# Shared network of a mixture-of-experts layer: the second product in plain fp32 instead of three passes over rounded and small parts

## The reference, cut to what matters

```python
SI = I * 2                     # I = 176
def _swiglu(gu, inter):
    g, u = (gu[..., :inter], gu[..., inter:])
    return jax.nn.silu(g) * u
...
y = jnp.einsum('eti,eih,te->th', h, w_down, combine)      # the experts
gu_s = x @ shared_gate_up                                  # 256 -> 2 * 352
y = y + _swiglu(gu_s, SI) @ shared_down                    # 352 -> 256
```

## Time and profile before

| | |
|---|---|
| time, median of 3 runs | 1204.62 us |
| lowest and highest | 1197.87 and 1205.65 us |
| span of the profiled execution | 1198.6 us |
| mean granted TensorE clock | 0.973 of full speed |
| PE busy | 1134.0 us (95%) |
| weight loads busy | 993.3 us (83%) |
| DVE busy | 756.3 us (63%) |
| ACT busy | 513.5 us (43%) |
| POOL busy | 240.8 us (20%) |

### The profile page before, as it was taken

The page is one execution under the profiler, slowest core; times in us unless marked ns, Lnnn a source line. Parts: engine busy times, 40 slices in busy tenths (PEclk is TensorE's granted clock), DMA queues, the critical chain, the costliest instruction groups (busy, mean ns, idle before and its releaser), DMA issues. The chain is left out here.

```text
span 1198.6 us, 19843 instructions
## 1 busy us (share of the span) xinstructions
PE 1134.0 (95%) x7044; PEld 993.3 (83%) x7044; DVE 756.3 (63%) x1600; ACT 513.5 (43%) x969; POOL 240.8 (20%) x274
## 2 busy tenths in 40 slices
PE   5999999999999999999999996889999779989997
PEld 4988988988989889889898995667776668878897
DVE  4765665666656647657567578754445975786656
ACT  5576344344443443444434555422222356554322
POOL 1012010110100101101001002033332742322211
PEclk9999999999999999999999997899999958999999
DMA  4001001000001001001000003733333324000001
GB/s 149 10 1 36 10 1 36 9 0 35 9 0 40 4 0 44 0 0 44 0 0 1 1 2 120 228 93 106 106 106 91 95 82 146 1 1 1 19 18 36
DMA packets 29212, 50.33 MB, mean 42 GB/s; under 512 B 5122, under 2 KB 19426, under 8 KB 27874
## 3 DMA queue, kind: packets, MB, share of 16 engines
q1 hardware_dynamic: 24978, 38.68, 9.8%
q0 software_dynamic: 3840, 10.49, 3.3%
q10 hardware_dynamic: 336, 0.39, 0.1%
HBM read 36.70 MB, written 10.49 MB: 39 GB/s over the span
## 5 line engine op out<-in xcount | busy, mean ns | idle before, releaser
L635 POOL TENSOR_TENSOR linear_out_row<-linear_out_row,lin_sq 128x512 f32<-128x512 f32 x64 | 91.3, 1426 | 598.7 <-ACT lin_sq L536 595.7
L42 PE MATMUL lin_bank<-keep_xT_hi,lin_w_hi 128*128 128x512 f32 x384 | 155.4, 405 | 2.6 <-DVE keep_xT_lo L244 2.6
L591 DVE TENSOR_TENSOR lin_st<-lin_bank,lin_mask 128x512 f32<-128x512 f32 x64 | 44.3, 692 | 174.9 <-PE lin_bank L446 174.9
L43 PE MATMUL lin_bank<-keep_xT_lo,lin_w_hi 128*128 128x512 f32 x384 | 152.6, 397 | 0.0
L44 PE MATMUL lin_bank<-keep_xT_hi,lin_w_lo 128*128 128x512 f32 x384 | 152.5, 397 | 0.0
L532 ACT ACTIVATE lin_o<-lin_bank 128x512 f32<-128x512 f32 x64 | 38.3, 598 | 189.9 <-PE lin_bank L477 189.9
L473 PE MATMUL lin_bank<-lin_st,lin_v 128*128 128x128 f32 x512 | 94.0, 275 | 0.0
L42 PEld LDWEIGHTS lin_bank<-keep_xT_hi,lin_w_hi 128*128 128x128 f32 x384 | 72.9, 190 | 17.9 <-issue 3.0
L44 PEld LDWEIGHTS lin_bank<-keep_xT_hi,lin_w_lo 128*128 128x128 f32 x384 | 72.5, 189 | 17.8
L477 PE MATMUL lin_bank<-lin_qd,lin_state 128*128 128x128 f32 x448 | 87.2, 276 | 0.0
L43 PEld LDWEIGHTS lin_bank<-keep_xT_lo,lin_w_hi 128*128 128x128 f32 x384 | 72.8, 189 | 14.8
(11 more groups left out here) (395 smaller groups left out, 2775.9 us busy)
## 6 DMA issues: line engine op xcount, KB each, us to landing
lin_raw<-in_wp SPq DMA_DIRECT2D x8, 1024.0 KB, 4.8
sorted_y<-shared_loaded SPq DMA_DIRECT2D x48, 128.0 KB, 2.1
experts_up_expert_up<-in_wgu SPq DMA_DIRECT2D x16, 352.0 KB, 7.2
keep_x<-in_x SPq DMA_DIRECT2D x4, 512.0 KB, 7.3
lin_raw_out<-in_wop SPq DMA_DIRECT2D x8, 256.0 KB, 2.6
tokens_x<-linear_out_row SPq DMA_DIRECT2D x4, 512.0 KB, 10.6
linear_out_row<-in_ffn_up SPq DMA_DIRECT2D x2, 1024.0 KB, 5.9
tail_q<-tail_qT SPq DMA_DIRECT2D x28, 64.0 KB, 2.0
```

The lines of the kernel that those rows point to most:

```text
L42: nc.tensor.matmul(out, lh, rh, start=first, stop=False, skip_group_check=skip)
L43: nc.tensor.matmul(out, lh, rl, start=False, stop=False, skip_group_check=skip)
L591: dve.tensor_tensor(C4(st[:, a, :]), C4(bank[2 + a][:]), mask[:, a:a + 1, :].broadcast_to([P, TPS, P]), ALU.mult).then_inc(st_sb, 1)
L635: pool.tensor_tensor(part, part, sq[:, a, :], ALU.add).then_inc(squares_sb, 1)
```

## The change

For the shared network, h and the down weights are no longer split. `pe_down_whole` multiplies h by the weights in plain fp32, one `matmul` for each tile of tokens where there were three. Gone are the roundings and rests of h (6 on ACT and 6 on DVE in the first place, 6 and 6, all on DVE, in the second), the three splits of down weights on ACT and DVE, and the buffers for them. The down weights get a tensor of their own (`d`), since routing reuses `loaded`. In return `h` has to live until its down product is done: `dve_product` of step n waits for `down_mm` of step n - 2, where it waited for the rest. In `experts` the product of step 5 moves behind `dve_tokens`. Buffers `h_hi` and `h_lo` shared their place in memory with `oP` in the tail; `oP` now has a place of its own. The feed-forward network keeps the three passes.

```diff
@@ SwigluWeights
-        if fetched is None:
+        self.whole_down = fetched is None
+        if self.whole_down:
             self.loaded = c.sb("loaded", [P, n_up + J * HID + LOADED_PAD])
-            fetched = Fetched(c, widths, self.loaded[:, 0:n_up], self.loaded[:, n_up:n_up + J * HID])
+            self.d = c.sb("d", [P, J, HID])
+            fetched = Fetched(c, widths, self.loaded[:, 0:n_up], self.d[:].rearrange("p j f -> p (j f)"))
...
-        self.d_lo, self.d_hi = c.sb("d_lo", [P, J, HID], F32R), c.sb("d_hi", [P, J, HID], F32R)
+        if not self.whole_down:
+            self.d_lo, self.d_hi = c.sb("d_lo", [P, J, HID], F32R), c.sb("d_hi", [P, J, HID], F32R)
@@ dve_product
         if n >= 2:
-            dve.wait_ge(self.h_sb, n - 1)
+            dve.wait_ge(self.down_mm, n - 1)
@@ new
+    def pe_down_whole(self, pe, g, j):
+
+        n, w = (g - self.start) * self.J + j, self.widths[j]
+        first, count = self.parts[g]
+        if n == 0 and not self.split_before:
+            pe.wait_ge(self.down_in, self.J * DMA)
+        pe.wait_ge(self.product_sb, n + 1)
+        for t in range(count):
+            to = self.bank[4 + (first + t) % TPS // 2][:, t % 2 * HID:(t % 2 + 1) * HID]
+            last = pe.matmul(to, self.h[0:w, n % 2, t * P:(t + 1) * P], self.raw_d[0:w, j, :],
+                             start=j == 0 and t % 2 == 0, stop=j == self.J - 1, skip_group_check=True)
         last.then_inc(self.down_mm, 1)
@@ experts, vector (excerpt)
                 net.dve_product(dve, *STEPS[4])
+                router.dve_tokens(dve, chain)
                 net.dve_product(dve, *STEPS[5])
-                router.dve_tokens(dve, chain)
-                net.dve_rest(dve, *STEPS[4])
                 router.dve_passed(dve, chain)
-                net.dve_rest(dve, *STEPS[5])
                 router.dve_tiles(dve, chain)
@@ window_attention, vector (excerpt)
-                net.dve_step(dve, chain, *STEPS[0])
-                net.dve_step(dve, chain, *STEPS[1])
+                net.dve_product(dve, *STEPS[0])
+                net.dve_product(dve, *STEPS[1])
                 weigh(a, 0, 1)
@@ window_attention, tensor
-                pe.wait_ge(net.h_sb, len(STEPS) - 1)
+                pe.wait_ge(net.product_sb, len(STEPS) - 1)
```

More of the change, by code:

```diff
@@ L969, in __init__ @@
         self.parts = {g: (g * TPS, TPS) for g in range(SEGS)}
-        self.raw, self.raw_d, self.w_lo, self.w_hi, self.d_lo, self.d_hi = w.raw, w.raw_d, w.w_lo, w.w_hi, w.d_lo, w.d_hi
+        self.whole_down = w.whole_down
+        self.raw, self.raw_d, self.w_lo, self.w_hi = w.raw, w.raw_d, w.w_lo, w.w_hi
         self.up_in, self.down_in, self.up_hi, self.down_hi, self.up_lo, self.down_lo = w.up_in, w.down_in, w.up_hi, w.down_hi, w.up_lo, w.down_lo
         self.silu, self.h = c.sb("silu", [P, 2, SEG]), c.sb("h", [P, 2, SEG])
-        self.h_hi, self.h_lo = place.sb("h_hi", [P, 2, SEG], F32R), place.sb("h_lo", [P, 2, SEG], F32R)
+        if not self.whole_down:
+            self.d_lo, self.d_hi = w.d_lo, w.d_hi
+            self.h_hi, self.h_lo = c.sb("h_hi", [P, 2, SEG], F32R), c.sb("h_lo", [P, 2, SEG], F32R)
         self.g_mm, self.u_mm, self.down_mm, self.silu_sb, self.product_sb, self.rounded, self.h_sb, self.y_sb = (
@@ L985, in act_high @@
             act.activation(self.w_hi[:, :, cols], self.raw[:, :, cols], ACT.Copy).then_inc(self.up_hi, 1)
+        if self.whole_down:
+            return
         act.wait_ge(self.down_in, self.J * DMA)
@@ L1039, in dve_product @@
         if n >= 2:
-            dve.wait_ge(self.h_sb, n - 1)
+            dve.wait_ge(self.down_mm, n - 1)
         dve.tensor_tensor(self.h[0:w, b, wide], self.silu[0:w, b, wide], self.bank[2 + b][0:w, wide], ALU.mult).then_inc(self.product_sb, 1)
-    def act_round(self, act, g, j):
-        n, w = (g - self.start) * self.J + j, self.widths[j]
-        b = n % 2
-        _, wide = self.tokens(g)
-        act.wait_ge(self.product_sb, n + 1)
-        if n >= 2:
-            act.wait_ge(self.down_mm, n - 1)
-        act.activation(self.h_hi[0:w, b, wide], self.h[0:w, b, wide], ACT.Copy).then_inc(self.rounded, 1)
-    def dve_rest(self, dve, g, j):
-        n, w = (g - self.start) * self.J + j, self.widths[j]
-        b = n % 2
-        _, wide = self.tokens(g)
-        h, h_hi, h_lo = (a[0:w, b, wide] for a in (self.h, self.h_hi, self.h_lo))
-        dve.wait_ge(self.product_sb, n + 1)
-        dve.wait_ge(self.rounded, n + 1)
-        dve.tensor_tensor(h_lo, h, h_hi.bitcast(F32), ALU.subtract).then_inc(self.h_sb, 1)
     def pe_up(self, pe, g, j):
@@ L1088, in pe_down @@
         b = n % 2
-        pe.wait_ge(self.rounded, n + 1)
-        if g == self.start and not self.split_before:
-            pe.wait_ge(self.down_lo, j + 1)
         if g > self.start and j == 0:
             pe.wait_ge(self.y_sb, 2 * min(g - self.start, SEGS - 1 - self.start))
+        if self.whole_down:
+            self.pe_down_whole(pe, g, j)
+            return
+        pe.wait_ge(self.rounded, n + 1)
+        if g == self.start:
+            pe.wait_ge(self.down_lo, j + 1)
         first, count = self.parts[g]
@@ L1107, in pe_down @@
             last = self.nc.tensor.matmul(to, h_lo[:, toks], d_hi, start=False, stop=j == self.J - 1, skip_group_check=True)
+        last.then_inc(self.down_mm, 1)
+    def pe_down_whole(self, pe, g, j):
[8 more added lines that the diff above has]
+                             start=j == 0 and t % 2 == 0, stop=j == self.J - 1, skip_group_check=True)
         last.then_inc(self.down_mm, 1)
@@ L1722, in _ @@
                 net.dve_product(dve, *STEPS[1])
-                net.dve_rest(dve, *STEPS[0])
                 router.dve_choose(dve, chain, 0)
@@ L2042, in window_attention @@
         bank = c.banks(8)
-        with Scope(nc, "tail_h") as c_h:
-            net = Swiglu(nc, c, keep, y, bank, SHARED, SHARED_EARLY, keep.shared, c_h)
-            net.split_before = True
+        net = Swiglu(nc, c, keep, y, bank, SHARED, SHARED_EARLY, keep.shared)
+        net.split_before = True
         oP = sb("oP", [P, BATCH, RR, WPAIRS * 2 * WIN])
@@ L2214, in _ @@
                 weigh(a, 2)
-                net.dve_step(dve, chain, *STEPS[2])
+                net.dve_product(dve, *STEPS[2])
                 weigh(a, 3, 4)
                 a.dve_known(dve, chain, "y")
-                net.dve_step(dve, chain, *STEPS[3])
+                net.dve_product(dve, *STEPS[3])
                 a.dve_x_by_tile(dve, chain)
-                net.dve_step(dve, chain, *STEPS[4])
+                net.dve_product(dve, *STEPS[4])
                 a.dve_apply(dve, "x", a.by_dve, a.z_dve)
-                net.dve_step(dve, chain, *STEPS[5])
+                net.dve_product(dve, *STEPS[5])
                 weigh(b, 0, 1)
```

14 lines of the change are left out of this document (3 added, 11 removed).

## The result

| | before | after |
|---|---|---|
| median of 20 runs each, same chip | 1200.49 us | 1196.4 us |
| lowest and highest | 1197.11 and 1205.65 us | 1193.57 and 1202.53 us |
| ratio, 95% interval | | 0.9964, 0.9954 to 0.9974 |
| span of the profiled execution | 1198.6 us | 1192.9 us |
| DVE busy / PE busy in the span | 756.3 / 1134.0 us | 744.7 / 1134.8 us |

The account below looks back on a forecast made before the run. DVE was taken as the fuller engine in routing and tail, the two stretches touched. Routing 0.5, clock 1.4 and tail 2.0 sum to 3.9 us, from a median of 1204.6 to 1200.7 us; range 1195 to 1208.

Parts of the forecast that it names:

- What PE pays: Down steps in routing and tail: a plain product costs 0.468 us against 0.357, so 0.44 us more a step.
- a price other than L2514's: Sign of being wrong: the plain down product costing other than L2514's 0.468 us.
- Routing, list: Routing up to the token list: PE takes over as the bound, so of 1.75 us on DVE 0.5 us remain.
- The product of step 3 hid its wait for down 1: Routing: DVE's new wait for down 1 hides with 0.5 us to spare; DVE waiting there would show the prediction wrong.
- the product of step 5 started at 790.92: Routing: this product needs down 3, done at 791.0, with the experts' table queued behind it to 794.2.
- Clock: After the gather: idle shrinks from 3.71 to 2.4 us and the clock stays up, -1.4 us, a little likelier than not.
- Tail: Tail up to L2021 and PE's wait at 957.43: DVE still decides, 2.0 us gained.
- The wait before L2413: Tail, L2418 in the kernel before: wait under 1 us, start 2.0 us earlier relative to the tail's first matmul.
- PE as the bound all along: Rival: PE's dearer product lies wholly on the path, twelve steps costing 5.3 us; chance 0.12.
- DVE's saving counting whole: Rival: all DVE work removed in routing and tail is gained, 10.5 us, giving 1194.1; chance 0.08.
- The clock rival: Rival: attention's clock recovers earlier or later (-2.5 or +2.5 us) or falls again (+4); 1199.6 to 1206.1, chance 0.18.

Follow-up runs that it names:

- dve_kept: Changed kernel with the subtractions and casts removed from DVE put back into an unread scratch buffer: -2.4 us (-4.8 to 0) against the kernel before.
- tail_only: Kernel before with the plain product in the tail alone, routing keeping three passes: -2.1 us (-3.9 to -0.2) against the kernel before.
- before_again: Kernel before, unchanged, traced again on the chip of the runs beside it: one execution at 1206.0 us, among runs of 1197.9 to 1206.9.
- after_again: Changed kernel, unchanged, run again beside the kernel before on the same chip: -3.8 us (-5.6 to -2.0) against the kernel before.
- reorder: Changed kernel with PE's two table products ahead of down 2, DVE's step 4 product behind the token list: -1.8 us (-3.7 to +0.1) against the kernel before.
- fill_route: Kernel before with 12 unused small PE products between the last down product and the first expert tile: -1.1 us (-2.5 to +0.2) against the kernel before.
- fill_start: Changed kernel with 7 unused small PE products behind the last expert tile: -6.3 us (-8.2 to -4.2) against the kernel before.
- fill_tail: Changed kernel with unused small PE products in the tail, 18 before and 6 behind the turning of v: -2.4 us (-4.2 to -0.6) against the kernel before.
- route_only: Kernel before with the plain product in the routing alone, tail keeping three passes: -3.0 us (-4.8 to -1.2) against the kernel before.

## Why the prediction was right, step by step

The median of the changed kernel, 1196.4 us, lies inside the range, but the range holds the kernel before's 1200.5 too, so that alone says little. The forecast's sum was 3.9 us and 4.3 were measured; the predicted median was 4.3 us too high because the three runs shown had a median of 1204.6 and twenty had 1200.5. The steps that it named are the ones that moved, but that the sum came so close is in part luck: terms too small and too large evened out, and one came true for another reason. The terms:

- **What PE pays: sized too dear.** 0.44 us a step was forecast from L2514. The plain down step takes 784.61 - 782.88 = 1.73 us, 0.432 a product, 0.30 a step more than three passes. The prediction had named a price other than L2514's as a sign of being wrong, and it was off by 0.04 us a product. More than half of this lies in the reading: within L2514 the entries start (1.94 - 0.38) / 7 = 0.223 us apart, 0.446 a product; the distance to the next instruction, of another shape, holds more.
- **Routing, list: right mechanism, 0.74 us for 0.49.** The ranks gained 0.81 (0.85 forecast), the idle of 0.54 closed, and the eight products cost 0.61 us and not 0.90: 0.81 + 0.54 - 0.61. PE took over as the bound, as said; `dve_kept` shows it (14.02 us with and without the rests) and DVE's 1.74 us of waiting. The product of step 3 hid its wait for down 1 at 780.71, and the product of step 5 started at 790.92 (791.0 forecast).
- **Gather: not foreseen.** The rows came 1.46 us sooner after the list. 0.42 of it is the issue, which holds in every trace. The landing after the issue, 4.84 us before and 3.80 after, is scatter: three traces with three passes have 3.8 to 4.8 us, eight with the plain product 3.4 to 5.6 (mean 4.1). So about 1 us of the traces' 5.7 probably belongs to the two executions and not to the change. That what is left is near the measured 4.3 proves little, since the clock moves single executions by 1 to 4 us, as above.
- **Clock: -1.3 us as forecast, for a reason that was half right.** The forecast's 1.4 us are the distance between the first two up products, 2.71 and 1.35 us. I expected 2.4 us of idle and that the clock would outlast it. The idle was 1.38, the first product 1.45 us. In the 14 traces the first tiles ran at full clock where PE had idled 0.5 to 1.8 us before (8 traces) and at 0.50, at least in part, where it had idled 2.0 to 5.2 us (6 traces, first up product 1.96 to 2.71 us). Had my 2.4 us come true, the term would likely have been zero (behind 2.02 and 2.69 us of idle the first up product took 2.56 and 1.96 us); it was saved by the gather, which I had not foreseen. That was luck.
- **Clock before the ranks: missed.** With three passes PE idles 2.0 us there; in four such traces the ranks' second group took 1.01, 1.01, 1.37 and 1.81 us. In the two slower ones, `tail_only` and `before_again`, the second table product comes 15.02 and 14.95 us behind the ranks and not 13.95, 1.0 us later. In the nine with the plain product the idle is 0.8 to 1.4 us and the group took 1.01 each time. So in some executions the change is worth 1 us more in the routing than these two profiles show. Two things shorten the idle: the choice comes 0.81 us earlier, and down 0 lasts 0.30 us longer. By the second the longer product pays back part of its price.
- **Tail: 2.30 us for 2.0.** Relative to the tail's first product, ACT's copy came 0.71 us later (1.1 forecast, again the price), the norm of y 0.79 us earlier (0.2), POOL's scale of x 0.84 earlier (0.5), DVE's L1929 0.98 earlier (0.65), and behind it rounding and rest gave 1.32 us (1.3). The wait before L2413 is 0.49 us, under 1 as said. The 2.30 us hold where the clock stays up at the tail's start. In `before_again` and `after_again` it fell there (first product 0.76 us), and the way to L2413 shrinks only from 36.63 to 35.55 us, by 1.08; PE, not DVE, is then what L2413 waits for in the changed kernel. `tail_only` (-2.1 us) agrees with the size, by an interval that nearly reaches zero; the cause rests on the traces, that of `dve_kept` above all.
- **Rivals.** PE as the bound all along, with 0.44 us for each of twelve steps, would have shown +5.3 us: ruled out. DVE's saving counting whole (-10.5): ruled out, by `dve_kept` and `reorder` for the routing. The clock rival did come into play: the attention's stretch at 0.50 ends 3 us later in the changed kernel, which costs 3.8 us of the lead, and the kernel before falls once more, which gives 3.6 back. In these two executions it nets to nearly zero by luck. What it does to the median is open: no run separates it, and since the second fall is in all four traces with three passes in the tail and in four of ten without, a part of the measured gain can be its.

## What to carry over

Between two engines that take turns, work taken off one is worth what the other leaves: here 0.7 of 1.75 us in the first stretch, 1.1 to 2.3 of 6.8 in the second, and each was fixed by naming the next wait on the other engine. Before moving work out of a gap, ask which wait the gap was covering (the copy to y in `reorder`), and whether the gap that is left can cost the clock: before the ranks a down step 0.30 us dearer left 0.80 us of idle and the clock alone, and one 1.25 us cheaper than that left 2.09 us, behind which the clock fell (PEclk 0.72 over the next 5.35 us), and gained nothing. Here a filler paid at most where the engine had no work to be late with and went on at a clock of 1.00 right behind (`fill_route`, `fill_start`); in `fill_tail` the second one took 2.93 us at 0.50.

## What the runs showed of the hardware

- Idle time of PE of 2.0 to 2.8 us went both ways with the clock. Behind the 2.00 us before the ranks it was 1.00 in `before` and 0.50 in `before_again` (second group 1.01 and 1.81 us), and the same 2.7 us before the tail took it in 5 of 12 traces with no filler near it (first product 0.76 us instead of 0.47) and not in the other 7. In two traces of the changed kernel the way to L2413 was 32.63 us with the clock kept and 35.55 with it lost, though that execution's other waits differ too. The clock also fell with next to no idle ahead: in the kernel before PE waits only once from 988 on, 0.25 us at 1000.04, and the clock is at 0.50 from about 1003 (1.00 over 1002 to 1003, 0.52 over 1003 to 1004). As an estimate from these (1.3 us in the first tiles, 2.9 us on the way to L2413, 3.6 us in the second fall), a good part of the 7 to 9 us by which executions of one kernel differ is of these kinds.
- In six of the 14 traces, all on chips where the kernel before takes 1207 to 1208 us, PE and DVE stand nearly still for several us, 15 to 20 us after the tail's start, with nothing to wait for that the profile shows. In `route_only` PE is busy 3.63 and DVE 1.03 of the 7.00 us from 935 to 942. PE there:

```profile
935.31 0.49 PE L43 MATMUL tail_bank<-keep_xT_lo,shared_w_hi 128*128 128x512 f32 x1 [0.32 <-issue]
936.72 0.39 PE L44 MATMUL tail_bank<-keep_xT_hi,shared_w_lo 128*128 128x512 f32 x1 [0.92 <-issue]
938.12 0.40 PE L42 MATMUL tail_bank<-keep_xT_hi,shared_w_hi 128*128 128x512 f32 x1 [1.01 <-issue]
939.52 0.58 PE L43 MATMUL tail_bank<-keep_xT_lo,shared_w_hi 128*128 128x512 f32 x1 [1.00 <-issue]
```

The way from the tail's first product to L2413 (or its like) is 38 to 43 us in these, 32 to 37 in the others, two of which have a gap of about 1 us at the same place. `before_again`, on a chip without it, can't tell whether chip or edit makes it, and what the engines wait for stays open.
